# Expert sums by transposes of 64 tokens on half arrays, with the turning banks shared and a new order

## What is computed

```
t = layernorm(token)
probs = softmax(t @ router_w + router_b)            # 8 experts
top_p, top_i = the two largest, scaled to sum to 1
y = sum over the two of top_p * (t @ expert_w[top_i] + expert_b[top_i])
out = token + y
```

## Time and profile before

| | |
|---|---|
| median of 3 runs | 1408.58 us (1408.44 to 1409.0) |
| the profiled execution | 1407.74 us, its span 1406.0 us |
| mean granted TensorE clock | 0.99 |
| busy: PE, DVE, ACT, POOL | 96%, 61%, 48%, 45% of the span |

### The profile page before, as it was taken

One profiled execution on the slowest core, in us unless ns is written; L12 is line 12 of the kernel. 1 busy time (PEld: TensorE's weight loads), 2 busy tenths in 40 slices (PEclk: granted clock), 3 DMA queues, 4 the chain that ended last, 5 costly groups with the idle time before them and its releaser, 6 DMA issues.

```text
span 1406.0 us, 30169 instructions
## 1 busy us (share of the span) xinstructions
PE 1345.1 (96%) x9344; PEld 1180.1 (84%) x9344; DVE 854.8 (61%) x1786; ACT 670.4 (48%) x2169; POOL 625.9 (45%) x752
## 2 busy tenths in 40 slices
PE   6899999999998999999999999979999999999997
PEld 5899999999998999999999999956666666666664
DVE  4788888755555222222222222269989989889896
ACT  5576777533434222222100000048778778778775
POOL 3566666100000000000144444457787887887886
PEclk9999999999999999999999999989999999999999
DMA  4112121100000000000011111100010100100101
GB/s 146 48 47 70 47 70 47 43 0 0 0 0 0 0 0 0 0 0 0 21 63 63 63 63 63 42 1 25 30 42 24 47 25 24 48 24 24 48 24 48
DMA packets 15372, 46.68 MB, mean 33 GB/s; under 512 B 2912, under 2 KB 2912, under 8 KB 15328
## 3 DMA queue, kind: packets, MB, share of 16 engines
q1 hardware_dynamic: 15184, 45.76, 9.3%
q10 hardware_dynamic: 144, 0.33, 0.1%
HBM read 31.33 MB, written 14.75 MB: 33 GB/s over the span
## 4 chain that ended last, share of the span: by engine, by line
PE 85%; DVE 6%; ACT 4%; issue 3%; POOL 1%; DMA 0%; DVEq 0%; POOLq 0%; ACTq 0%
PE twin L951 33%; PE twin L868 26%; PE twin L1007 9%; PE twin L1019 6%; PE twin L974 5%; PE twin L859 2%; PE twin L853 2%; PE twin L988 2%; ACT late L506 1%; DVE parts L732 1%; DVE scratch L792 1%; ACT more L506 1%; DVE act_buf L800 1%; ACT parts L491 1%; DVE twin L750 0%
## 5 line engine op out<-in xcount | busy, mean ns | idle before, releaser
L951 PE MATMUL twin<-kbuf,late 128*128 128x136 f32 (+2 forms) x3940 | 458.2, 280 | 5.0 <-DVE kbuf L700 5.0
L951 PEld LDWEIGHTS twin<-kbuf,late 128*128 128x128 f32 x3940 | 458.0, 192 | 5.3 <-DVE kbuf L700 5.3
L868 PE MATMUL twin<-parts 128*128 128x384 f32 (+2 forms) x2070 | 392.8, 341 | 0.0
L868 PEld LDWEIGHTS twin<-parts 128*128 128x128 f32 x2070 | 371.2, 188 | 2.8 <-issue 2.5
L297 POOL TENSOR_TENSOR act_buf<-kbuf,x_in 128x144 f32 (+1 forms) x198 | 96.6, 488 | 564.8 <-DVE kbuf L706 564.8
L706 DVE SCALAR_TENSOR_TENSOR kbuf<-twin,act_buf 128x144 f32<-128x144 f32 x394 | 121.3, 308 | 337.2 <-PE twin L951 337.2
L1007 PE MATMUL twin<-em,parts 64*128 64x512 f32 x1404 | 227.7, 429 | 5.0 <-DVE scratch L792 2.7
L322 POOL TENSOR_TENSOR scratch<-scratch 128x512 f32<-128x512 f32 x126 | 160.7, 1278 | 53.7 <-ACT scratch L506 36.7
L473 ACT ACTIVATE x_in<-twin 128x384 f32<-128x384 f32 (+1 forms) x90 | 40.3, 447 | 302.0 <-PE twin L974 302.0
L1007 PEld LDWEIGHTS twin<-em,parts 64*128 64x128 f32 x1404 | 116.7, 186 | 55.0 <-issue 36.7
L459 ACT ACTIVATE act_buf<-kbuf 128x144 f32 x196 | 63.2, 323 | 167.5 <-DVE kbuf L706 167.5
(11 more groups left out here) (102 smaller groups left out, 1535.8 us busy)
## 6 DMA issues: line engine op xcount, KB each, us to landing
x_in<-x SPq DMA_DIRECT2D x36, 400.0 KB, 3.5
x_in<-x_col SPq DMA_DIRECT2D x20, 720.0 KB, 4.1
result<-act_buf SPq DMA_DIRECT2D x36, 400.0 KB, 2.8
scratch<-L_conv_w_d ACTq DMA_DIRECT2D x1, 320.0 KB, 4.7
scratch<-L_conv_w_u SPq DMA_DIRECT2D x1, 320.0 KB, 6.1
late<-L_conv_w_r SPq DMA_DIRECT2D x1, 320.0 KB, 6.4
late<-L_conv_w_l SPq DMA_DIRECT2D x1, 320.0 KB, 7.2
ew<-L_ffn_expert_w SPq DMA_DIRECT2D x2, 128.0 KB, 6.2
```

Source lines behind the costliest of these rows:

```text
L868: last = mm(acc[:, lo:hi], vw[:, k, wpart, si], carry[:, cpart, g, lo + s * BG:hi + s * BG], start=first and si == 0, stop=final and si == ...
L951: last = mm(banks[CONV[g]][:, lo * BG:hi * BG], hw[:, k, si], kbuf[:, g, lo + s:hi + s].rearrange("p j b -> p (j b)"), start=si == 0, stop ...
```

## The change

- `sum_experts`: each of the four 128x128 transposes becomes two, on the lower and the upper 64 partitions (64 tokens each), with a 64x64 piece of the identity. The two write to different banks, 4 and 5 (SUMS), 64 columns each. `add_out` reads both banks.
- `tokens` and `channels` now share one bank, CTB (7), and wait for each other's readers.
- Two more staging buffers, in the place of `sq`, `lnv` and `rstd` (one tensor, `spare`), six in all. The sums follow their tile by three (LAG = 3).
- ACT_TILES is 7 to 12: tile 6 is wholly DVE's.
- The places of all steps stand in tables (TURN_AT for `tokens`, COPY_AT, VAR_AT, INV_AT, SCALE_AT, BACK_AT for `channels`, HIGH_AT and LOW_AT for the two parts, STEP_AT, EXP_AT), as (tile, place), where place 0 is ahead of the tile's main item, 1 behind it, and on PE and DVE 2 behind the sum or the addition.
- COPY_TILES is empty; its branches do nothing.

```diff
+        spare = sb("spare", [P, 3 * 2 * NC])
+        sq, lnv, rstd = (spare[:, 2 * NC * k:2 * NC * (k + 1)].rearrange("p (b n) -> p b n", b=2) for k in range(3))
+        gated = [scratch[:, 0:E * P], scratch[:, E * P:2 * E * P], late[:, 0:E * P], more[:, :],
+                 spare[:, 0:E * P], spare[:, E * P:2 * E * P]]
-        CT, TB = 4, 5
-        LOG, SUM = 6, 7
+        SUMS, LOG, CTB = [4, 5], 6, 7
-        FILL_CT, FILL_TB = [4, 0, 1, 2, 3], [5, 7, 5, 7, 5]
-
-        ACT_TILES = (6, 7, 8, 9, 10, 11, 12)
+        FILL_CT, FILL_TB = [7, 0, 1, 2, 3], [4, 5, 7, 4, 5]
+
+        ACT_TILES = (7, 8, 9, 10, 11, 12)
+        COPY_TILES = ()
-        LAG = 2
+        LAG = 3
-            return k % 4 if k < SEQ - 6 else (k - (SEQ - 6)) % 3
+            return k if k < 6 else (k - 6) % 5
-        STEP_AT = [(6, 2), (7, 0), (7, 1), (7, 2), (8, 0), (8, 1), (8, 2), (9, 0), (9, 2), (10, 0), (10, 1), (10, 2),
-                   (11, 0), (11, 1), (11, 2), (12, 0), (12, 1)]
+        TURN_AT = [(0, 0), (1, 1), (2, 1), (3, 1), (5, 0)]
+        COPY_AT = [(0, 1), (0, 1), (2, 1), (3, 0), (3, 1)]
+        VAR_AT = [(0, 2), (1, 2), (2, 1), (3, 1), (5, 0)]
+        INV_AT = [(2, 0), (3, 0), (3, 0), (4, 1), (5, 0)]
+        SCALE_AT = [(1, 1), (3, 1), (3, 1), (5, 0), (5, 0)]
+        BACK_AT = [(5, 1), (6, 1), (7, 1), (8, 2), (10, 0)]
+        HIGH_AT = [(5, 0), (5, 1), (6, 0), (7, 1), (9, 0)]
+        LOW_AT = [(5, 1), (6, 1), (7, 2), (9, 0), (9, 2)]
+        STEP_AT = [(7, 0), (7, 2), (8, 0), (8, 2), (9, 0), (9, 1), (9, 1), (9, 2), (10, 1), (10, 2), (11, 0), (11, 1), (11, 2), (11, 2), (12, 0), (12, 0), (12, 2)]
+        EXP_AT = (11, 0)
...
             def region(j, slot, now):
 
                 for p in range(TILES):
-                    if now is not None:
-                        if p == EXP_TILE:
-                            exponential(now)
-                        if 5 <= p < NCK + 5:
-                            first_part(now, 1 - slot, p - 5)
-                        if p < NCK:
-                            copy_tokens(now, 1 - slot, p)
-                    if p in ACT_TILES:
-                        gate_odd(j, slot, p)
-                    if now is not None and 1 <= p < NCK + 1:
-                        inv_std_tokens(now, 1 - slot, p - 1)
+                    for place in range(2):
+                        if place == 1 and p in ACT_TILES + COPY_TILES:
+                            gate_odd(j, slot, p)
+                        if now is not None:
+                            if EXP_AT == (p, place):
+                                exponential(now)
+                            for c in at(HIGH_AT, p, place):
+                                first_part(now, 1 - slot, c)
+                            for c in at(INV_AT, p, place):
+                                inv_std_tokens(now, 1 - slot, c)
+                            for c in at(COPY_AT, p, place):
+                                copy_tokens(now, 1 - slot, c)
...
-                width, off = (QUAD * TN, 0) if hi < TILES else (TAIL, TN - TAIL)
-                dst = flat(j)[:, lo * TN:lo * TN + width]
                 dve.wait_ge(s_y, TILES * j + hi)
-                nc.vector.tensor_tensor(dst, banks[SUM][:, off:off + width], dst, ALU.add).then_inc(s_o, 1)
+                if hi < TILES:
+                    dst = flat(j)[:, lo * TN:hi * TN].rearrange("p (t r n) -> p r t n", r=2, n=C)
+                    src = twin[SUMS[0] // 2][:, :, 0:(hi - lo) * C].rearrange("p r (t n) -> p r t n", n=C)
+                    nc.vector.tensor_tensor(dst, src, dst, ALU.add).then_inc(s_o, 1)
+                else:
+                    dst = flat(j)[:, REG - TAIL:REG]
+                    nc.vector.tensor_tensor(dst, banks[SUMS[1]][:, 0:TAIL], dst, ALU.add).then_inc(s_o, 1)
...
-                at = (p % QUAD) * TN
-                for e in range(E // 2):
-                    last = mm(banks[SUM][:, at:at + TN], stage(slot, p)[:, e], ident[:, :],
-                              start=e == 0, stop=e == E // 2 - 1, is_transpose=True)
+                col, count = (p % QUAD) * C, E if p in COPY_TILES else E // 2
+                for e in range(count):
+                    for r in range(2):
+                        half = slice(r * C, (r + 1) * C)
+                        last = mm(banks[SUMS[r]][:, col:col + C], stage(slot, p)[half, e], ident[half, half],
+                                  start=e == 0, stop=e == count - 1, is_transpose=True)
                 last.then_inc(s_y, 1)
 
             def region(j, slot, now):
                 for p in range(TILES):
-                    experts(j, slot, p)
-                    if now is not None:
-                        if 5 <= p < NCK + 5:
-                            channels(now, 1 - slot, p - 5)
-                        if p < NCK:
-                            tokens(now, 1 - slot, p)
-                    if p >= LAG:
-                        sum_experts(j, slot, p - LAG)
-                    elif later(j):
-                        sum_experts(j - 1, 1 - slot, TILES + p - LAG)
+                    for place in range(3):
+                        if place == 1:
+                            experts(j, slot, p)
+                        elif place == 2:
+                            if p >= LAG:
+                                sum_experts(j, slot, p - LAG)
+                            elif later(j):
+                                sum_experts(j - 1, 1 - slot, TILES + p - LAG)
+                        if now is not None:
+                            for c in at(BACK_AT, p, place):
+                                channels(now, 1 - slot, c)
+                            for c in at(TURN_AT, p, place):
+                                tokens(now, 1 - slot, c)
```

More of the change, by code:

```diff
@@ L122, in act_gates @@
         def act_gates(j, p):
-            return len(ACT_TILES) * j + sum(a <= p for a in ACT_TILES)
+            tiles = ACT_TILES + COPY_TILES
+            return len(tiles) * j + sum(a <= p for a in tiles)
         bias_row = banks[LOG][:, 2 * NSM + 3 * NG:2 * NSM + 3 * NG + E]
@@ L139, in stage_age @@
             k = TILES * slot + p
-            return next(d for d in range(1, SEQ) if stage_of(k - d) == stage_of(k))
+            return next(d for d in range(1, SEQ + 1) if stage_of(k - d) == stage_of(k))
         def tiles_of(c):
@@ L153, in metaformer_kernel, with at @@
         EX_STEP = 12
[L155 to L157 removed]
+        TURN_AT = [(0, 0), (1, 1), (2, 1), (3, 1), (5, 0)]
[8 more added lines that the diff above has]
+        EXP_AT = (11, 0)
+        def at(table, p, place):
+            return [c for c, when in enumerate(table) if when == (p, place)]
         s_wd = sem("s_wd")
@@ L339, in region @@
                 for p in range(TILES):
-                    if now is not None and 2 <= p < NCK + 2:
-                        scale_tokens(now, 1 - slot, p - 2)
-                    pair_sums(j, slot, p)
+                    for place in range(2):
+                        if place == 1:
+                            pair_sums(j, slot, p)
+                        if now is not None:
+                            for c in at(SCALE_AT, p, place):
+                                scale_tokens(now, 1 - slot, c)
             for c in range(NCK):
@@ L765, in softmax_steps, with softmax @@
                 ]
[L767 to L778, removed]
+            def softmax(j, slot, k):
+                if k == 0:
+                    dve.wait_ge(s_xn2, NCK * (j + 1))
+                elif k == EX_STEP:
+                    dve.wait_ge(s_ex, j + 1)
+                if k > 0:
+                    dve.wait_ge(s_sm, SMN * j + k)
+                softmax_steps(j, slot)[k]().then_inc(s_sm, 1)
             def gate_tile(j, slot, p):
@@ L813, in region @@
                 for p in range(TILES):
-                    if now is not None and 1 <= p < NCK + 1:
-                        square_sums(now, 1 - slot, p - 1)
-                    gate_tile(j, slot, p)
-                    if now is not None and 5 <= p < NCK + 5:
-                        second_part(now, 1 - slot, p - 5)
-                    for part in range(3):
-                        if part == 2:
+                    for place in range(3):
+                        if place == 1:
+                            gate_tile(j, slot, p)
+                        elif place == 2:
                             add_behind(j, p)
                         if now is not None:
-                            softmax(now, 1 - slot, (p, part))
+                            for c in at(VAR_AT, p, place):
+                                square_sums(now, 1 - slot, c)
+                            for c in at(LOW_AT, p, place):
+                                second_part(now, 1 - slot, c)
+                            for k in at(STEP_AT, p, place):
+                                softmax(now, 1 - slot, k)
             for c in range(NCK + 2):
@@ L829, in _ @@
                     second_part(0, 0, c - 2, FILL_TB[c - 2])
```

(9 more changed lines are left out.)

50 lines of the change are left out of this document (32 added, 18 removed).

## The result

| | before | after |
|---|---|---|
| median | 1408.79 us (1408.44 to 1411.4, 4 runs) | 1375.53 us (1374.99 to 1377.58, 4 runs) |
| ratio | | 0.9763, 95% interval 0.9746 to 0.978 |
| the profiled execution, its span | 1407.74 us, 1406.0 us | 1375.32 us, 1373.5 us |
| mean granted TensorE clock | 0.99 | 0.989 |

The account below looks back on a forecast made before the run. PE and DVE together were taken to bound a 26.0 us region. At 25.1 it saves 17 x 0.9 = 15.3, the last region about 2: -17.3 on the profiled 1407.74 gives 1390.4, median 1391; range 1376 to 1414.

Parts of the forecast that it names:

- S: One tile's sum on PE, eight half-array transposes: 0.43 us, pairs 0.107 apart by the weight load; bounds 0.21 to 0.87.
- E itself: A tile's six expert matmuls on PE, without the cost of changing tiling: 3 x 0.23 = 0.69 us.
- rival D: On PE, no drain is saved between sums and experts: period 26.4 us, 1414 us; chance 0.05.
- T and B: PE's turning of three tiles and transposing three back, alone among 64-row groups, pay on both sides: 1.12 and 0.67 us.
- The walk: One region's cycle: ACT late from tile 7's experts to tile 1's, 11.9 us, then PE 12.7; together 24.6.
- E7: Tile 7's six expert matmuls on PE: from their end on ACT was forecast to be the late engine.
- E1: Tile 1's six expert matmuls on PE: forecast to start 11.9 us into the cycle, PE late from there, 12.7.
- LAG 3 and six buffers take stage waits away; the trace shows few, nothing: Sums three tiles behind and six staging buffers: few stage waits to remove, so no gain.
- Rival E: The waits vanish: 24.2 us a region, 1376 us; chance 0.10.
- A: Rival: in the sums on PE the two halves do not run together, +2.5 us a region, 1452 us; chance 0.08.
- C: Rival: DVE keeps the period at 25.9 to 26.1 us, 1405 to 1409 us; chance 0.11.
- B: Rival: ACT's high parts before gates wait for PE, ACT later at tile 12: period 26.3 and more, 1412 us; chance 0.11.

Follow-up runs that it names:

- s_w64: The kernel before with turning and transposes back sharing one bank, its sums' full-array transposes loading 64 of 128 weight columns: 1406.23 us.
- a_w64: The changed kernel, its half-array transposes loading 64 of the 128 weight columns: 1373.12 us.
- lag3_only: The kernel before with shared turning bank, LAG 3 and six staging buffers, old sums and order kept: 1409.39 us, 0.9993.
- a_act6: The changed kernel with tile 6 given back to ACT (ACT_TILES 6 to 12): 1423.37 us, 1.0089.
- half_spread: The kernel before with half-array sums, shared turning bank, LAG 3, six buffers, and transposes back moved behind tiles 5, 6, 8, 10, 12: 1397.42 us, 0.9905.
- half_lag3: The kernel before with half-array sums, shared turning bank, LAG 3 and six buffers, old order and ACT tiles: 1400.94 us, 0.9932.

## Why the prediction was wrong

- **S, "4 x 0.107 = 0.43" by "I stay by the load": the term that failed.** It measures 0.27: one step of 0.11, then two of 0.06, then 0.03 until E. Its lower bound, 0.21, was nearer. I held that the load sets the pitch of a pair and that E's pairs show it, but no row there does: the earlier trace rows have only the first two loads, and E's pairs, of 512 columns, come 0.24 apart. The loads of E are not transposing ones either; the 141 ns of L1019 stood in the same view as the 184 of L1007, and two of L1019's loads 0.06 apart in the same trace. What sets the pitch is the stream, but for the first pair (s_w64, a_w64). The Trainium skill (TensorE: Matmul & The Clock Gate, LDWEIGHTS) gives a load by its column count alone, which makes 107 ns of 128 columns (an estimate by that page's formula) and with it the forecast's 0.107; here two loads of 128 columns differ as 141 and 189 ns, pairs of them follow each other 62 ns apart, and the measurement decides.
- **E itself, 0.69**, is 0.77 to 0.79 until the next S: its second pair still comes 0.30 to 0.33 behind the first, where I had 0.23. That its load is not covered by so short a transpose is my reading, not shown. E+S came to 1.04 for 1.12. That no drain stands between them held: S starts 0.23 after E's last pair, the pitch inside E, where other tilings wait 0.32; so rival D falls. T and B stayed expensive on both sides, as said: E to T 0.88, T to S 0.93, B to S 0.45 to 0.48.
- **PE's work**, with these: 13 x 1.04 + 4 x 1.05 (T) + 0.52 + 4 x 0.60 (B) + 0.4 = 21.0 a region for the forecast's 22.8; the busy time went from 24.63 to 21.80.
- **The walk held.** ACT's arc, from E7's end (1165.57 + 0.9) to E1 (1178.33), is 11.8 for 11.9. That it comes out so close is in part luck: PE's own chain, which I had end it, is now done some 0.3 earlier, and ACT's gate of tile 12, forecast and measured at 11.7, holds E1. PE's arc, from E1 on: three T tiles of 2.09, 1.56 with the one-tile T (1184.60 to 1186.16), 1.64 for a B tile, 1.92 for the next with its wait, 0.9 for E7, 12.3 in all. Without the one wait of 0.26 it is 12.0, for 12.7. So of the missing microsecond a region, 0.7 is S, and T and B beside it, and 0.25 is the allowance of 0.5 for short waits, of which B1's 0.26 is all that came. DVE's chain from step 1 to tile 0's gate is 11.1 for 11.0.
- **"LAG 3 and six buffers take stage waits away; the trace shows few, nothing": failed as a statement.** It is right of the kernel before (lag3_only, 0.9993) and wrong of the change (some 30 and 13 us). The walk assumed that no sum ever waits, and this is what buys it. The short sums alone bring 7 us, everything else alone 6; all of it is 33.
- **Rival E's number, 24.2 and 1376, came out by luck, its reason did not**: PE's waits for ACT and DVE did not vanish, they grew from 1.1 to 2.1 us a region; it was the work that shrank. A falls (pairs run together), C falls (DVE's period fell with the rest to 24.15, though it is busy for 96% of it). B did not happen, but was one tile away.

**What to carry to other kernels.** Where two instructions of one kind stand in a view with different lengths, take the one that does what the new instruction will do, and look for the shortest distance at which two of them start. Compare two orders region by region, with the clock beside each region, before the medians are read. Price a lag, a buffer or a place in the kernel as it will be, not as it is: in a ring that several engines hold, each relief alone is worth little and one of them left out costs nearly all. Before handing a tile to another engine, look at what stands in front of it in that engine's queue.

## What the hardware showed beside

- **Half-array transposes in pairs.** Two fp32 transposes, on the lower and upper 64 rows, into two banks, start 3 to 4 ns apart, the second pair 0.11 behind the first and the later ones 0.06: eight take 0.27 us where four on the full array take 0.53. Half of it is gained, since half the columns are streamed. In every sum behind T or B the first two start so; in 81 of the 127 sums behind an E they start some 30 ns apart, one by one, and the pace is the same.
- **The clock after a wait.** In a_act6 PE waits 1.77 us, and its clock falls to the lower level, 1.2 GHz, for 6 to 7 us. In half_spread it did so in one of two regions, behind a wait of 1.54 us for the addition (the number before the last two is the clock, its mean over the window; full is 1.00):
```profile
1160.00:1164.00 4.00, 2.46 (x31) 1.69 (x30) 3.90 (x11) 4.00 (x21) 2.71 (x3) 1.00 0.00 0
1164.00:1168.00 4.00, 4.00 (x25) 2.79 (x21) 3.33 (x7) 2.13 (x11) 2.69 (x3) 0.58 0.01 4
...
1188.00:1192.00 4.00, 2.43 (x31) 1.60 (x29) 3.90 (x11) 3.58 (x19) 2.79 (x3) 1.00 0.00 0
1192.00:1196.00 4.00, 3.99 (x42) 2.87 (x40) 3.74 (x7) 2.53 (x10) 2.86 (x3) 1.00 0.02 4
```
The second region of that trace has the same wait, 1.57 us, and keeps the full clock: a wait of this length is a risk, not a rule. Shorter ones carry it too. In half_lag3, behind waits of 0.60 and 1.03 us that end at 1138.07 and 1140.07, the clock is low from about 1140.6 on:
```profile
1142.00:1144.00 2.00, 2.00 (x12) 1.31 (x10) 1.54 (x4) 1.56 (x8) 1.02 (x2) 0.51 0.00 0
```
while nine other regions of the same trace keep it. Each fall costs 1.2 to 1.6 us there and in half_spread.
